# Attention loop of a decoder layer: other PSUM banks, other places for projection parts, VectorE adds a sixth of the row sums

## The reference

```python
qkv = x @ qkv_w + qkv_b                                   # q, k, v: 16 heads of 32
attn = jnp.einsum('bnhd,bmhd->bhnm', q, k) * scale
attn = jax.nn.softmax(attn, axis=-1)
out = jnp.einsum('bhnm,bmhd->bnhd', attn, v).reshape(b, n, c)
```

## Time and profile before

| | us |
|---|---|
| median of 3 runs | 3649.93 |
| lowest and highest run | 3646.7 and 3657.5 |
| span of the profiled execution | 3644.6 |
| TensorE busy in it | 3423.0 (94%) |
| VectorE busy | 2510.0 (69%) |
| GpSimd busy | 1995.2 (55%) |
| ScalarE busy | 1672.6 (46%) |

### The profile page before, as it was taken

The page is one execution under the profiler, slowest core; times in us unless marked ns, Lnnn a source line. Parts: engine busy times, 40 slices in busy tenths (PEclk is TensorE's granted clock), DMA queues, the critical chain, the costliest instruction groups (busy, mean ns, idle before and its releaser), DMA issues. The chain is left out here.

```text
span 3644.6 us, 50074 instructions
## 1 busy us (share of the span) xinstructions
PE 3423.0 (94%) x18021; PEld 2227.0 (61%) x18021; DVE 2510.0 (69%) x4512; ACT 1672.6 (46%) x3043; POOL 1995.2 (55%) x1008
## 2 busy tenths in 40 slices
PE   7999999999999999999999987999959899999996
PEld 5545455455455555455454435877739789988885
DVE  5777777777777777777777735889834765566667
ACT  2455555555555555555555553444312333233332
POOL 2688888888888888888898950011110101110112
PEclk9999999999999999999999998999969999999998
DMA  6322221321312312213120022132132333323332
GB/s 223 103 56 65 86 62 62 93 67 61 97 50 73 97 50 85 73 50 106 56 64 24 15 93 66 58 121 81 53 119 81 113 113 104 116 89 114 117 128 99
DMA packets 190278, 308.49 MB, mean 85 GB/s; under 512 B 25514, under 2 KB 72234, under 8 KB 190011
## 3 DMA queue, kind: packets, MB, share of 16 engines
q1 hardware_dynamic: 166970, 243.82, 21.8%
q0 software_dynamic: 14592, 44.32, 3.5%
q10 hardware_dynamic: 8448, 16.78, 1.3%
HBM read 195.66 MB, written 61.33 MB: 71 GB/s over the span
## 5 line engine op out<-in xcount | busy, mean ns | idle before, releaser
L511 DVE TENSOR_REDUCE sa_part_max<-sa_mx 128x1 f32<-128x512 f32 x2048 | 1282.4, 680 | 539.8 <-PE sa_mx L625 536.0
L466 ACT ACTIVATE sa_prob<-sa_sc 128x512 f32<-128x512 f32 x2010 | 1101.3, 595 | 803.7 <-PE sa_sc L692 764.4
L268 POOL TENSOR_TENSOR sa_quad_sum<-sa_quad_sum,sa_prob 128x1024 f32<-128x1024 f32 x500 | 1174.6, 2382 | 6.3 <-ACT sa_prob L466 6.3
L268 POOL TENSOR_TENSOR sa_quad_sum<-sa_prob 128x1024 f32<-128x1024 f32 x250 | 588.2, 2372 | 266.9 <-ACT sa_prob L466 266.9
L2055 PE MATMUL ex_h<-ex_xT,ex_w 128*128 128x384 f32 (+2 forms) x2688 | 463.9, 328 | 52.0 <-issue 24.4
L625 PE MATMUL sa_mx<-sa_k_even,sa_q_stack 96*128 96x512 f32 x1024 | 490.8, 483 | 17.2 <-DVE sa_part_max L511 7.5
L625 PE MATMUL sa_mx<-sa_k_odd,sa_q_stack 96*128 96x512 f32 x1024 | 476.6, 465 | 10.0 <-DVE sa_part_max L511 8.6
L2055 PEld LDWEIGHTS ex_h<-ex_xT,ex_w 128*128 128x128 f32 x2688 | 445.3, 194 | 64.8 <-issue 32.6
L692 PE MATMUL sa_sc<-sa_q_stack,sa_k_even 98*128 98x512 f32 x1024 | 427.1, 417 | 0.0
L2066 PE MATMUL ex_acc<-ex_w,ex_hT 128*128 128x512 f32 x1719 | 415.6, 392 | 1.9 <-DVE ex_hT L1994 1.6
L692 PE MATMUL sa_sc<-sa_q_stack,sa_k_odd 98*128 98x512 f32 x986 | 415.5, 423 | 1.6 <-ACT sa_prob L466 1.6
(11 more groups left out here) (229 smaller groups left out, 3776.8 us busy)
## 6 DMA issues: line engine op xcount, KB each, us to landing
ex_w_in<-in_L_ffn_w_dram SPq DMA_DIRECT2D x130, 512.0 KB, 4.1
sa_xT<-xT SPq DMA_DIRECT2D x57, 1024.0 KB, 5.1
sa_q_stack<-sa_hilo SPq DMA_DIRECT2D x372, 64.0 KB, 2.0
rows<-sa_empty SPq DMA_DIRECT2D x48, 257.0 KB, 3.7
ex_rows<-rows POOLq DMA_DIRECT2D x8, 1542.0 KB, 7.7
sa_k_odd<-sa_hilo SPq DMA_DIRECT2D x192, 64.0 KB, 2.0
ex_xg<-rows POOLq DMA_DIRECT2D x48, 256.0 KB
sa_k_even<-sa_hilo SPq DMA_DIRECT2D x168, 64.0 KB, 2.0
```

The source lines that it names most:

```text
L268: pool.tensor_tensor(quad_sum[:, i % 2, heads, :], so_far, prob[:, k, heads, :], ALU.add).then_inc(quad_ready, 1)
L466: act.activation(prob[:, kt % 4, j, :], score_bank(n)[:, :], ACT.Exp, scale=SCALE).then_inc(prob_ready, 1)
L511: dve.reduce_max(part_max[:, q, j, k:k + 1], mx[n % 3][:, :], AX_X).then_inc(max_read, 1)
```

## The change

- The bank den is given up: row sums collect in misc, between the jobs of projections. Its place becomes a third score bank, so a score waits for the exponential three before it.
- Two of a chunk's four row sums run in step 15 (of its quads 0 and 1), the others in steps 1 and 2 of the next chunk; quad_sum has four slots.
- The parts of projections stand in odd steps 3 to 13, two in each: one after head 1, one after the last head. Their results are left in steps 6, 10 and 14 (before: 4, 8, 12).
- ScalarE takes the high part of Q and K (`leave_high_part`), ahead of the exponential of head 1.
- VectorE adds heads 2 and 3 of the first two steps of each quad (`add_pair`, in steps 2, 6, 10 and 14, after the second maximum); GpSimd has five additions per quad instead of six, and its third waits for VectorE's.
- VectorE's reciprocals stand in steps 4 and 8, two each, in place; the copy of the row sums goes into recip and waits for the store of the chunk before. GpSimd's division goes from (quad 1, step 1) to (quad 2, step 2), the store from step 10 to 13.
- The shift is transposed in a turn of the maxima's three banks; its copy is made in step 13 and its rows are moved in step 14.
- q_stack has three slots of 512 queries instead of 2048 columns.

The diff, cut to its core:

```diff
-    QUADS, ADDS = T // 4, 6
-    DEN_LAG = 6
+    QUADS, ADDS = T // 4, 5
+    PAIR_AT = (2, 6, 10, 14)
+    HIGH_HEAD = 1
+    Q_SLOTS = 3
+    OWN_SUMS_AT, PREV_SUMS_AT = {15: (0, 1)}, {1: (2,), 2: (3,)}
-    SUMS_AT, DENS_AT, DIVIDE_AT, STORE_AT = 0, 2, (1, 1), 10
-    INVERT_AT = ((3, 1), (3, 3), (4, 1), (4, 3))
+    SUMS_AT, DENS_AT, DIVIDE_AT, STORE_AT = 0, 2, (2, 2), 13
+    INVERT_AT = (4, 4, 8, 8)
-    PARTS_AT = ((0, 1, 2, 3), (4, 5, 6, 7), (8, 9, 10, 11))
+    PARTS_AT = ((3, 3, 5, 5), (7, 7, 9, 9), (11, 11, 13, 13))
...
-    quad_sum = s.sb("quad_sum", [P, 2, HG, BANK])
+    quad_sum = s.sb("quad_sum", [P, QUADS, HG, BANK])
-    sc = [s.ps(f"sc{i}") for i in range(2)]
+    sc = [s.ps(f"sc{i}") for i in range(3)]
-    den = s.ps("den")
+    den = misc
...
             for half in range(2):
+                if (k, half) == (1, 1):
+                    continue
                 pool.wait_ge(prob_ready, (g * T + 4 * i + k) * HG + 2 * half + 2)
-                if k > 1:
-                    pool.wait_ge(quad_ready, d * ADDS + 2 * (k - 1) - 1 + half)
+                if (k, half) == (2, 1):
+                    pool.wait_ge(pair_ready, d + 1)
+                elif k > 1:
+                    pool.wait_ge(quad_ready, d * ADDS + (1 if k == 2 else 2 + half))
...
+        def leave_high_part(i):
+            job, order = JOBS[i], SPLITS.index(i)
+            act.wait_ge(proj_mm, i + 1)
+            before = SPLITS[order - 2]
...
+                act.wait_ge(stacked[JOBS[before].what, JOBS[before].n], stacked_by(before))
+            bias = qkb[:, 0 if job.what == "q" else 1, job.unit % G:job.unit % G + 1]
+            act.activation(hilo[:, order % 2, 0, :], misc[:, :], ACT.Identity, bias=bias).then_inc(hi_ready, 1)
...
         def leave_den(g):
             act.wait_ge(den_mm, (g + 1) * QUADS)
-            after(act, recip_ready, TQ * g)
-            act.activation(dens[:, :], den[:, :], ACT.Copy).then_inc(dens_ready, 1)
+            if g > 0:
+                act.wait_ge(attn_out[(g - 1) % 2], ((g - 1) // 2 + 1) * 16)
+            act.activation(recip[:, :], den[:, :], ACT.Copy).then_inc(dens_ready, 1)
...
+        def add_pair(g, i):
+            d = g * QUADS + i
+            after(dve, den_mm, d - QUADS + 1)
+            dve.wait_ge(prob_ready, (g * T + 4 * i + 2) * HG)
+            dve.tensor_tensor(quad_sum[:, i, 2:4, :], prob[:, 0, 2:4, :], prob[:, 1, 2:4, :], ALU.add).then_inc(pair_ready, 1)
...
                     if i == 1 and (g, kt) in LEAVE_AT:
                         leave_psum(LEAVE_AT[g, kt])
-                    if (kt, i) in INVERT_AT and g > 0:
-                        invert(g - 1, INVERT_AT.index((kt, i)))
+                    if i == 1 and kt in PAIR_AT:
+                        add_pair(g, PAIR_AT.index(kt))
+                    for q in range(TQ):
+                        if i == 1 and kt == INVERT_AT[q] and g > 0:
+                            invert(g - 1, q)
...
-            if kt % 4 == DEN_LAG % 4 and step >= DEN_LAG:
-                if kt == DEN_LAG:
-                    after(pe, dens_ready, g)
-                row_sums((step - DEN_LAG) // 4)
+            for i in PREV_SUMS_AT.get(kt, ()) if g > 0 else ():
+                row_sums((g - 1) * QUADS + i)
+            for i in OWN_SUMS_AT.get(kt, ()):
+                before = [job for (chunk, step), job in LEAVE_AT.items() if chunk == g]
+                if i == 0 and before:
+                    pe.wait_ge(v_ready if JOBS[before[-1]].what == "v" else hilo_ready, left_psum(before[-1]))
+                row_sums(g * QUADS + i)
...
-            after(pe, prob_ready, n - 4 if n >= LAST * T * HG + len(last_sc) else n - 1)
+            after(pe, prob_ready, n + 1 - (len(last_sc) if n >= FIRST_LAST + len(last_sc) else len(sc)))
...
-                        if i == 1 and kt % 2 == 0:
+                        if i == 1:
                             burst(g, kt)
...
-                if (g, kt) in PART_AT:
-                    project_part(*PART_AT[g, kt])
+                    parts = PART_AT.get((g, kt), ())
+                    if i == 1 and len(parts) == 2:
+                        project_part(*parts[0])
+                if parts:
+                    project_part(*parts[-1])
```

More of the change, by code:

```diff
@@ L129, in self_attention @@
     VALUES = [i for i, job in enumerate(JOBS) if job.what == "v"]
-    PART_AT = {(job.chunk, kt): (i, part) for i, job in enumerate(JOBS) if job.place for part, kt in enumerate(job.place)}
+    PART_AT = {}
+    for i, job in enumerate(JOBS):
+        for part, kt in enumerate(job.place or ()):
+            PART_AT.setdefault((job.chunk, kt), []).append((i, part))
     LEAVE_AT = {(job.chunk, job.place[-1] + 1): i for i, job in enumerate(JOBS) if job.place}
@@ L145, in stacked_by, with turn_of, shift_turn, turn_left @@
                         if (other.what, other.n) == (JOBS[i].what, JOBS[i].n))
+    def turn_of(n):
+        return n + max((n - SHIFT_TURN) // NMAX, 0)
+    def shift_turn(g):
+        return (g + 1) * NMAX + SHIFT_TURN + g
+    def turn_left(engine, turn):
+        users = turn // (NMAX + 1) + 2
+        shifts = [g for g in range(users) if shift_turn(g) == turn]
+        if shifts:
+            engine.wait_ge(shiftT_ready, shifts[0] + 1)
+        elif turn >= 0:
+            engine.wait_ge(max_read, min(turn - sum(1 for g in range(users) if shift_turn(g) < turn) + 1, CHUNKS * NMAX))
+    def maximum_at(g, kt, i):
+        n = (g + 1) * NMAX + LEAD + kt * PER_STEP + i
+        return [n] if n < CHUNKS * NMAX else []
     def job_of(unit, what, n):
@@ L496, in leave_psum @@
             bias = qkb[:, 0 if job.what == "q" else 1, job.unit % G:job.unit % G + 1]
-            if job.place is not None:
-                before = SPLITS[order - 2]
-                if JOBS[before].place is None:
-                    stacked_first(dve, JOBS[before].what, JOBS[before].n)
-                else:
-                    dve.wait_ge(stacked[JOBS[before].what, JOBS[before].n], stacked_by(before))
-                dve.tensor_scalar(hilo[:, order % 2, 0, :], bank[:, :], bias, None, ALU.add).then_inc(hi_ready, 1)
             dve.wait_ge(hi_ready, order + 1)
@@ L603, in project_part @@
                     after(pe, in_x[slot], 16 * loads_until(job.load))
-                if not first and i == 0 or not first and JOBS[i - 1].chunk != job.chunk:
-                    pe.wait_ge(shiftT_ready, job.chunk + 1)
+                if not first and JOBS[i - 1].chunk != job.chunk:
+                    if job.chunk > 0:
+                        pe.wait_ge(dens_ready, job.chunk)
                 elif not first or i >= 3:
```

104 lines of the change are left out of this document (58 added, 46 removed).

## The result

| | before | after |
|---|---|---|
| median, us | 3651.7 (4 runs, 3646.7 to 3657.5) | 3826.95 (4 runs, 3809.1 to 3831.0) |
| ratio | | 1.047 [1.0445, 1.0495] |
| span of the profiled execution, us | 3644.6 | 3822.7 |
| mean granted clock | 0.972 | 0.948 |

The changed kernel is 175 us slower. The span grew by 178, and the attention loop carries all of it: from the first maximum of one chunk to that of the next, a mean of 65.03 us became 70.84, and 5.8 x 31 = 180.

The account below looks back on a forecast made before the run. TensorE was taken to bound the attention loop, with some 6% short bank waits. Span 3644.6 - 121 (removed waits) + 183 (stalls) + 56 (clock) = 3763, hence a 3768 us median; range 3595 to 3830.

Parts of the forecast that it names:

- the clock: Attention loop: TensorE's idling in two stalls per chunk lowers the granted clock, 0.9 us each, +56 us (0 to 205).
- removed waits, less the row sums alone: Attention loop: 4.2 us of TensorE's bank waits vanish per chunk, less 0.3 for row sums standing alone: -121 us.
- stalls behind the pair, steps 7, 11, 15: TensorE waits for VectorE's reads, delayed by the pair addition standing behind GpSimd's: 5.9 us per chunk, +183 us.
- The order in Q and K steps: Steps with a Q or K job: GpSimd's addition starts 0.13 us before VectorE's pair addition; TensorE stalls 2.15 us.
- Behind V jobs: Steps with a V job, one of three: GpSimd first by 0.36 us, TensorE stalls 1.6 us.
- Step 2: No job there: VectorE free after 1.22 us, ahead of GpSimd's 1.5, so no stall (0.85 if late).
- Edits at nothing: High part on ScalarE, shift, moves, store and division, charged nothing; moves 0 to 1.5 us in half the chunks.
- Rival 1: VectorE starts first with Q and K, only V jobs stall: 3579 us, up to 3644, middle 3610; chance 0.26.
- the surcharge: VectorE-first case: late GpSimd meets the small L520 after step 12, up to 1.6 us per chunk; moves up to 0.5.
- Rival 2: No exclusion between the pair addition and GpSimd's additions: 3530 to 3550 us; chance 0.10.
- Rival 3: Half the removed waits return as waits for VectorE: 3830 us with stalls, 3590 without (0.04).
- Rival 4: Every stall drops the clock and step 2 stalls too: +26 + 149, 3900 us at most; chance 0.06 shared.

Follow-up runs that it names:

- one input: Changed kernel with VectorE's pair addition replaced by a maximum over the same 1024 columns of one SBUF tile, row sums left incomplete: 3548.9 us, 0.9717.
- stall filled: Changed kernel with the first score of steps 7, 11 and 15 run seven times, so TensorE has work during most of the wait: 3750.0 us, 1.0264.
- the kernel with the early pair: Changed kernel with VectorE's pair addition after the first maximum of its step instead of after the second and the projection's leave: 3577.1 us, 0.9799.
- six additions: Changed kernel with all six additions of a quad on GpSimd again and no pair addition on VectorE: 3628.0 us, 0.9934.
- short additions: Changed kernel with each of GpSimd's additions cut into two of one head, 512 columns each: 3678.7 us, 1.0071.
- the run with the pair ahead of the job: Changed kernel with VectorE's pair addition still after the second maximum but before the projection's leave: 3630.5 us, 0.9943.

## Why the prediction was right, and where its sum was off

The forecast of 3768 had the right sign and cause; the time was 59 us more, 3 us below the upper end of its range. That it lies inside is partly luck: 3830 was the clock at twice its price (3768 + 56 = 3824, rounded up), and the clock gave only about 21 of the 59. Three kernels split the result into the forecast's own terms, one by one: with no collision (one input) the change gives 3548.9 - 3651.7 = -103; with the collisions but no lost clock (stall filled) 3750.0 - 3548.9 = +201; the clock 3827.0 - 3750.0 = +77. Of the 201, step 3 has 0.83 x 31 = 26, and the table gives the rest to steps 7, 11 and 15. The step times of the two traces agree roughly: 24 for step 3 and 171 for the other three, of which 8 are the repeats of the last three chunks, so that the stalls have rather 163 to 167 and the clock 77 to 85.

| term, us | forecast | runs |
|---|---|---|
| removed waits, less the row sums alone | -121 | -103 |
| stalls behind the pair, steps 7, 11, 15 | +183 | +175 |
| stall in step 3 | 0 | +26 |
| clock | +56 | +77 |
| together | +118 | +175 |

- **The order in Q and K steps: right.** GpSimd was forecast 2.9 and VectorE 3.0 after the step's begin; in step 6 above it is 846.83 - 844.01 = 2.82 and 3.02. The pair's end came at 6.28 (forecast 6.35) and the stall was 2.13 (2.15). Between the two kernels of the +201, steps 7, 11 and 15 differ by 1.96, 2.02 and 1.73 on average (5.26, 5.65 and 5.70 against 3.30, 3.63 and 3.97), 5.7 a chunk where the forecast had 5.9. Behind V jobs (step 7 of every fourth chunk) it is 4.86 against 3.19, 1.67 where 1.6 was forecast.
- **Step 2: the step that failed.** The forecast let VectorE be free 1.22 after it began the first read, two reads, ahead of GpSimd's 1.5. It left out that the read of step 1's last maximum is still queued: three reads, and VectorE is late by 0.03. The price that the forecast set for that case, 0.85, was measured as 0.83.
- **The clock: right in kind, small in size.** A quarter of a full drop was charged for each of 62 stalls. The loop has 44 half-speed stretches, and 77 / 44 = 1.75 us for each: fewer drops than stalls, each about half of the 3.3 us that the earlier trace rows gave, since 36 of these stretches last 3.4 us and not 6.7.
- **Removed waits: 18 too much.** The row sums that stand alone cost more than the 0.3 charged. In the kernel with the early pair a row sum inside a burst costs step 2's 4.78 less step 0's 3.92, 0.86; alone, step 1 takes 3.07 - 1.88 = 1.19, 0.33 more, and step 15 with two 3.93 - 1.88 = 2.05, again 0.33 more. So 0.66 per chunk: 11 of the 18. The wait for moved rows, put at nothing or up to 1.5 in half of the chunks, is 5.9 us on TensorE in the one-input kernel and 19.6 in the one with the early pair.
- **Edits at nothing: two were not.** "An engine that nobody waits for here" was true of GpSimd in the kernel before: in the faster loop its sixth addition costs 51 us. The high part's move was charged nothing as a cost, and rightly, but it gives 36 us, part of the removed term that the forecast did not tell apart.
- **Rivals.** Rival 1 (VectorE first) did not happen. The kernel with the early pair comes nearest to it, and its 3577.1 beside the rival's 3579 (before the surcharge) is a coincidence: the 3579 has 50 us of stalls behind V jobs, which this kernel doesn't have. Without them the rival's sum is 3529, and the kernel is 48 above it: the 18 of the removed waits, and 28 between this kernel and the one-input kernel. The surcharge, for moved rows and for the small operations, shows in steps 12 and 13, which are 0.48 and 0.42 longer than in the one-input kernel; both are under the 0.5 and 1.6 set as their most, and only with six additions does the second reach 2.2. Rival 2 (no exclusion) falls by 3.26 against 1.21. Rival 3 (waits come back whatever happens) falls by the one-input kernel: the same VectorE work and 103 us gained. Rival 4 was half right: step 2 does stall, but not every stall drops the clock; its own sum, 3768 + 26 + 149, is 3943 and not "3900 at most".

## What to carry to other kernels

When work moves to VectorE, ask whether its operands lie in SBUF while GpSimd adds there: a wide addition of two tiles and a tensor_scalar of 16 columns both stood, a reduction of one tile and an operation with one of its two inputs in PSUM did not. Small operations belong in that list: with six additions on GpSimd two of 16 columns, and what waits for them, cost 51 us. If it may stand, list the starts of both engines in each place and put VectorE's operation into a pause of GpSimd, not where a tenth of a microsecond decides. Count into those starts every read still queued from the step before. A stall of about 2 us can cost more than its length when TensorE idles through it (77 us over 44 drops of the clock here): fill it, or, better, move what causes it.

## What the runs showed of the hardware that was not expected

- **A waiting VectorE operation does not always get in between two GpSimd additions.** With six additions, the shift's operation of 16 columns began at 410.26, while GpSimd ran the second of two until about 411.3 and the next one from there to 413.62; it ended at 413.66. In the kernel before, one that began at 1980.02 got in at such a boundary, at about 1981.1, and with short additions the pair got in between two of them (2.14 on average, and not 1.21 + 2 x 1.28). What decides is open.

```profile
410.26 3.40 DVE L560 TENSOR_SCALAR sa_shift<-sa_top 128x16 fp32r<-128x16 f32 x1
```
```profile
406.62 4.71 POOL L298 TENSOR_TENSOR sa_quad_sum<-sa_quad_sum,sa_prob 128x1024 f32<-128x1024 f32 x2
411.29 2.33 POOL L298 TENSOR_TENSOR sa_quad_sum<-sa_prob 128x1024 f32<-128x1024 f32 x1
```

- **Start order is decided within 0.03 us**, and the later one stands for the whole of the other's instruction (829.54 and 829.57 in step 2 above, 411.46 and 411.51 in the run with the pair ahead of the job).
- **More matmuls made the kernel faster**: 31 x 3 x 6 repeated scores, 558 in all, gave 77 us back, since the granted clock stayed at 1.00, the 2.4 GHz level, over 200 to 2050 us.
